# Work moved at five places of a hand-ordered layer kernel: pads, the first attention's start and steps, the second's steps and ends

## The chip, the cores and the metric

The kernel runs on one core of a Trainium2 chip. The metric is the device time of one execution in microseconds (us). Its engines are named as in the profile: PE is the matrix engine, PEld its weight loads, DVE, ACT and POOL are the vector, scalar and GpSimd engines, SP issues most DMAs.

## The reference

The inputs are x (32 batches of 112 tokens, 512 wide), a memory of 32 x 375 x 256, a mask that names one of two experts for each token, and weights. All of it is float32.

```python
# layer 0: attention over the memory, gated
memory_proj = einsum('bme,de->bmd', memory, W_mem)
attn = softmax(einsum('bnd,bmd->bnm', x, memory_proj) / sqrt(512))
context = einsum('bnm,bmd->bnd', attn, memory_proj)
gate = sigmoid(concat([x, context]) @ W_gate + b_gate)
h = rmsnorm(x + gate * context, norm_w)
# layer 1: two experts, chosen per token by vm
n = rmsnorm(h, ln_in_w)
q, k, v = split(where(vm, n @ v_qkv, n @ l_qkv))      # 16 heads of 32
ctx = softmax(causal(rope(q) @ rope(k).T)) @ v
h = h + where(vm, ctx @ v_dense, ctx @ l_dense)
cq = rmsnorm(h, ln_post_cross_w) @ cq_w               # 16 heads of 16
ck, cv = split(memory @ ckv_w)
h = h + softmax(cq @ ck.T) @ cv @ cdense_w            # 375 keys
m = rmsnorm(h, ln_post_attn_w)
return h + where(vm, v_mlp(m), l_mlp(m))              # silu(gate) * up, down
```

## The kernel before

The order of every engine is written out by hand. The blocks at the end of the program (@block.sync, gpsimd, scalar, tensor, vector) call, one after the other, a function per phase and engine (a_sp, a_pool, a_act, a_pe, a_dve, then b_..., to f_...). An instruction waits on semaphores; nothing reorders. A product of two float32 matrices is three matmuls of high and low halves (split_products, lines L111 to L113). The low halves are made by L179 on DVE or POOL.

- **Phase a** (0 to 325 us) computes layer 0 in 8 groups of 4 batches. For group g PE makes u(g), the scores, the gate products, transposes the probabilities (transposed, L681, onto PSUM) and multiplies them with the memory (attended, L689). DVE copies the turned probabilities out of PSUM (attended, L796), splits them (attended_low), blends gate and input (gated, L784 and L787) and writes the normed rows (tokens, L822). Setup work for the later routing by expert is threaded into the first groups on DVE: setup_dve_places after u_low of group 1, setup_dve_slots after the softmax of group 1. The routing sorts the 3584 tokens into 28 blocks of 128 slots plus two pad blocks: DVE computes the pads' slots in nine small instructions (L422 to L430), and POOL scatters pad rows into three tables in DRAM (L271 to L273).
- **Phase b** (to about 590 us) is the norm, qkv and rope in 8 tiles of up to 512 slots; POOL scatters the rows of q, k and v back to token order by indirect DMA (store_qk, store_v L970). The semaphore b_v_scattered counts landings of v rows. POOL waits before the last tile's scatters until all earlier ones have landed.
- **Phase c** (to about 775 us) is self-attention, one batch a step s: PE runs masks and scores (L1311, L1321) of batch s, the transposes of the probabilities (L1332) and the contexts (L1343) of batch s - 1. DVE takes maxima (L1393) and subtracts them (shift, L1402) into c_prob, ACT takes the exponent in place (L1261) and copies turned queries and keys (L1225, L1229) and turned probabilities (L1248). The first shift waits in DVE's order for the v scatters, since its destination shares their storage.
- **Phase d** is the dense product, residual and queries; phase f is the MLP in tiles.
- **Phase e** (937 to 1447 us) is cross-attention in 34 steps s. A step holds for batch s the scores (L2017, units 0 to 5, whose maxima DVE takes with L2159), for batch s - 1 the scores by key (L2038, exponents on ACT L1906), for batch s - 2 the contexts (L2051, the output in tiles of 32 columns of the array, two calls t = 0, 1), their turn (L2068) after a copy by ACT (L1912), the norm (DVE L2192, L2194), back (L2074) and the dense product. The maxima of batch s - 1 are turned by one transpose (maximum_turn, L2063), copied by DVE (L2176) and placed by a DMA of SP (L1812) into a row that the scores by key of that batch read. SP also issues the placing of keys (L1766) and queries (L1808) per batch. The key products of batch s + 2 (e_key_products) and its turned queries (queries_turn) stand in the same step.

Of the kernel before, what the change touches and what calls it, by code (L numbers as in the profile page):

```python
# [16 lines left out]
NB = 4  # L17
# [98 lines left out]
def build_xattn(nc, x_t, mem_t, mem_n, mem_e, weights, e_weights, q_weights, w_gate_mem, w_mem, b_gate,  # L116
# [3 lines left out]
    with ExitStack() as ctx:  # L120
# [137 lines left out]
        def setup_pool(pool):  # L258
            pool.memset(minus_half[:], -0.5).then_inc(s_pool, 1)
            pool.iota(row_i, pattern=[[0, SEQ]], base=0, channel_multiplier=1).then_inc(s_pool, 1)  # L260
            for m in range(RING):
                if m == C_GATE:
                    pool.wait_ge(a_m_lo, 2 * CT)
                ring_low(pool, m)
            pool.memset(tok[:, 0:PADS, :], 0.0).then_inc(pads_zeroed, 1)
            pool.wait_ge(pads_zeroed, 1)
            pool.memset(tok[:, PADS:NB, DIM:ROW], 0.0).then_inc(pads_zeroed, 1)
# [116 lines left out]
        def setup_dve_places(dve):  # L384
# [5 lines left out]
            for x, whole in enumerate((full, shift)):  # L390
                one_by_one(dve, dve.tensor_scalar(beyond[:, WHOLE * x:WHOLE * x + WHOLE], end_of, whole, None, ALU.is_gt))
            dve.wait_ge(s_rank, 2)
# [13 lines left out]
        def setup_dve_slots(dve):  # L406
# [14 lines left out]
            grid = consts[:, 8:8 + PADS]  # L421
            one_by_one(dve, dve.tensor_tensor(gap, full, count_sb, ALU.subtract))  # L422
            one_by_one(dve, dve.tensor_scalar(pads_inside, gap, -1.0, None, ALU.mult))
            one_by_one(dve, dve.tensor_tensor(pads_inside, gap, pads_inside, ALU.max))
            one_by_one(dve, dve.tensor_scalar(gap, pads_inside, -1.0, None, ALU.mult))
            one_by_one(dve, dve.tensor_scalar(pad_m, grid, pads_inside, None, ALU.is_lt))
            one_by_one(dve, dve.tensor_scalar(pad_m, pad_m, gap, float(TOKENS), ALU.mult, ALU.add))
            one_by_one(dve, dve.tensor_tensor(pad_slot[:], pad_m, grid, ALU.add))
            dve.wait_ge(pads_zeroed, 2)
            dve.tensor_scalar(tok[:, 0:PADS, ID].bitcast(I32), grid, float(TOKENS), None, ALU.add).then_inc(slots_made, 1)  # L430
# [313 lines left out]
        def a_dve(dve):  # L744
# [91 lines left out]
            for g in range(GROUPS + 1):  # L836
# [10 lines left out]
                if g < GROUPS:  # L847
                    for b in range(NB):
                        if b + 2 < NB:
                            attended(g, b + 2)  # L850
                        attended_low(g, b)
                        if g and b == 1 and g + 1 < GROUPS:
                            memory_low(g + 1, 1)
                if g:
# [4 lines left out]
                    means(g - 1, 1)  # L859
                    tokens(g - 1, 0)  # L860
# [39 lines left out]

        b_vs_last = [fv(at, (VROW,)) for at in (19248, 20336)]
# [57 lines left out]
        def b_pool(pool):  # L959
# [28 lines left out]
            pool.wait_ge(b_v_scattered, 16 * blocks(TILES - 1))  # L988
# [152 lines left out]
        c_q_t, c_k_t = ([fv(at + 448 * i, (KT, SEQ)) for i in range(2)] for at in (7728, 15872))  # L1141
        c_prob = [fv(10496 + 1792 * i, (HEADS, SEQ), SEQ) for i in range(2)]
        c_prob_t, c_ctx_raw = fv(14080, (HEADS, SEQ), SEQ), fv(16768, (KT, SEQ))
        c_tok = [fv(17216 + 512 * i, (DIM,), SEQ) for i in range(2)]
# [7 lines left out]
        def c_sp(sp):  # L1152
# [14 lines left out]
            sp.wait_ge(b_v_scattered, 16 * BLOCKS)  # L1167
# [21 lines left out]
        def c_pool(pool):  # L1189
# [5 lines left out]
            def fold(b):  # L1195
                pool.wait_ge(c_exp, b + 1)
                if b == 0:
                    pool.wait_ge(b_v_scattered, 16 * BLOCKS)
# [23 lines left out]
        def c_act(act):  # L1222
# [19 lines left out]
            for s in range(BATCHES + 1):  # L1242
# [12 lines left out]
                if s + 2 < BATCHES:  # L1255
                    keys(s + 2)
# [1389 lines left out]
```

## Time and profile before

| | us |
|---|---|
| median of 3 runs | 2146.66 |
| lowest and highest | 2146.21, 2147.8 |
| the profiled execution | 2143.99 |
| its span in the trace | 2142.2 |
| PE busy | 2093.4 (98% of the span) |
| POOL, DVE, ACT busy | 943.5, 1237.3, 1050.2 |

Of the span 1.8 us of the execution lie around it. The mean granted clock of PE on the page is 0.993. The page's last chain of waits lies on PE for 83% of the span. A wait in the trace names what ended last before an instruction could start.

### The profile page before, as it was taken

The numbers are of one execution on the slowest core, as the hardware profiler recorded it, in microseconds if no ns is written. First come the engines' busy times: TensorE is split into PE (matmuls) and PEld (weight loads), VectorE is DVE, ScalarE is ACT, GpSimd is POOL, SyncE is SP. The second block draws the span as 40 slices with busy tenths as digits, with TensorE's granted clock in tenths as the row PEclk, the third lists the DMA queues.
The fourth block names the chain that finished last, engine by engine and source line by source line (L and its number), as shares of the span: only waits on it lengthen the run. The fifth ranks groups of instructions, "written<-read, shape, count | busy, mean of one in ns | idle before, by whom it ended". The sixth has DMA issues, their size and how long they took to land.

```text
span 2142.2 us, 40674 instructions
## 1 busy us (share of the span) xinstructions
PE 2093.4 (98%) x16042; PEld 1805.2 (84%) x16042; DVE 1237.3 (58%) x1908; ACT 1050.2 (49%) x1877; POOL 943.5 (44%) x773
## 2 busy tenths in 40 slices
PE   8999999999999999999999999989999999999998
PEld 7899998888777778887888888878888888888888
DVE  6665547657589975456666666663434435344343
ACT  5444435343378865534666565553443434433334
POOL 2211127776668854551111211115455554555447
PEclk9999999999999999998999999999999999999999
DMA  6443435655666655567877777745335343443334
GB/s 248 140 158 115 144 134 177 228 204 212 212 202 181 186 189 216 227 201 212 238 235 210 226 217 222 207 132 188 116 122 174 112 140 111 131 142 118 115 89 134
DMA packets 155742, 373.00 MB, mean 174 GB/s; under 512 B 40384, under 2 KB 61216, under 8 KB 145824
## 3 DMA queue, kind: packets, MB, share of 16 engines
q1 hardware_dynamic: 136400, 310.18, 45.8%
q0 software_dynamic: 18720, 60.04, 7.6%
q8 instruction: 128, 2.10, 0.4%
q14 instruction: 62, 0.51, 0.1%
q10 hardware_dynamic: 432, 0.17, 0.0%
HBM read 268.70 MB, written 100.46 MB: 172 GB/s over the span
## 4 chain that ended last, share of the span: by engine, by line
PE 83%; DMA 5%; DVE 3%; POOL 3%; SPq 2%; ACT 2%; issue 1%; POOLq 0%; DVEq 0%; ACTq 0%
PE ps L111 20%; PE ps L113 20%; PE ps L112 20%; PE ps L2017 4%; PE ps L2038 4%; PE ps L2051 3%; PE ps L1332 2%; PE ps L689 2%; PE ps L1321 1%; PE ps L1343 1%; DMA f_arena<-weights 1%; POOL cq_rows L1569 1%; PE ps L1311 1%; DMA cq_rows<-f_arena 1%; ACT f_arena L1595 1%
## 5 line engine op out<-in xcount | busy, mean ns | idle before, releaser
L111 PE MATMUL ps<-r_arena 128*128 128x512 f32 (+6 forms) x2410 | 890.9, 370 | 14.0 <-DVE r_arena L179 8.9
L113 PE MATMUL ps<-r_arena 128*128 128x512 f32 (+6 forms) x2410 | 880.0, 365 | 0.0
L112 PE MATMUL ps<-r_arena 128*128 128x512 f32 (+6 forms) x2410 | 879.6, 365 | 0.0
L179 POOL TENSOR_TENSOR r_arena<-f_arena,r_arena 128x512 fp32r<-128x512 f32 (+1 forms) x434 | 576.7, 1353 | 542.1 <-ACT r_arena L201 397.3
L111 PEld LDWEIGHTS ps<-r_arena 128*128 128x128 f32 (+2 forms) x2410 | 453.1, 188 | 79.0 <-POOL r_arena L179 6.7
L113 PEld LDWEIGHTS ps<-r_arena 128*128 128x128 f32 (+2 forms) x2410 | 452.7, 188 | 64.9
L112 PEld LDWEIGHTS ps<-r_arena 128*128 128x128 f32 (+2 forms) x2410 | 453.7, 188 | 59.3
L201 ACT CAST r_arena<-f_arena 128x512 fp32r<-128x512 f32 x400 | 236.4, 624 | 172.5 <-PE ps L113 127.3
L2159 DVE TENSOR_REDUCE e_negmax<-ps 112x3 f32<-112x1125 f32 (+1 forms) x192 | 229.9, 1198 | 113.1 <-PE ps L2017 113.0
L2476 DVE SCALAR_TENSOR_TENSOR f_arena<-f_arena,ps 128x512 f32<-128x512 f32 (+1 forms) x88 | 57.5, 653 | 233.8 <-ACT f_arena L2363 233.8
L1906 ACT ACTIVATE f_arena<-ps 125x896 f32<-125x896 f32 x192 | 165.4, 915 | 35.6 <-PE ps L2038 33.0
L2367 ACT CAST r_arena<-ps 128x512 fp32r<-128x512 f32 (+1 forms) x88 | 49.3, 561 | 240.1 <-DVE ps L2480 240.1
L1864 POOL DMA_INDIRECT cd_rows<-f_arena,slot_all x32 | 30.0, 937 | 268.2 <-ACT f_arena L1961 268.0
L2017 PE MATMUL ps<-r_arena 96*112 96x376 f32 x512 | 134.6, 358 | 9.7 <-DVE e_negmax L2159 4.5
L179 DVE TENSOR_TENSOR r_arena<-ps,r_arena 128x512 fp32r<-128x512 f32 (+2 forms) x186 | 102.6, 563 | 71.6 <-ACT r_arena L2367 55.1
L2480 DVE SCALAR_TENSOR_TENSOR ps<-f_arena,ps 128x512 f32<-128x512 f32 (+1 forms) x88 | 58.3, 663 | 103.9 <-PE ps L113 103.6
L2363 ACT ACTIVATE f_arena<-ps 128x512 f32<-128x512 f32 (+1 forms) x88 | 50.2, 571 | 133.0 <-PE ps L113 133.0
L2038 PEld LDWEIGHTS ps<-r_arena 98*125 98x125 f32 x768 | 99.5, 192 | 15.3 <-ACT f_arena L1906 9.9
L2038 PE MATMUL ps<-r_arena 98*125 98x224 f32 x768 | 110.4, 281 | 1.8 <-DMA r_arena<-r_arena 0.8
L2017 PEld LDWEIGHTS ps<-r_arena 96*112 96x112 f32 x512 | 81.9, 184 | 24.9 <-DVE e_negmax L2159 13.7
L518 POOL TENSOR_TENSOR a_rstd<-a_ss,minus_half 112x2 f32<-112x2 f32 x16 | 11.3, 705 | 194.8 <-DVE a_ss L806 194.7
L1202 POOL TENSOR_TENSOR f_arena<-f_arena 112x896 f32<-112x896 f32 x32 | 66.9, 2090 | 34.6 <-ACT f_arena L1261 32.7
(215 smaller groups left out, 2575.4 us busy)
## 6 DMA issues: line engine op xcount, KB each, us to landing
f_arena<-weights SPq DMA_DIRECT2D x400, 256.0 KB, 3.0
r_arena<-k_rows SPq DMA_DIRECT2D x192, 188.0 KB, 3.6
k_rows<-r_arena SPq DMA_DIRECT2D x64, 376.0 KB
f_arena<-rows SPq DMA_DIRECT2D x14, 1160.0 KB, 5.2
f_arena<-qk_rows SPq DMA_DIRECT2D x32, 448.0 KB, 4.1
f_arena<-mem_n SPq DMA_DIRECT2D x8, 1536.0 KB, 6.8
f_arena<-mem_e SPq DMA_DIRECT2D x32, 376.0 KB, 4.9
f_arena<-mem_t SPq DMA_DIRECT2D x16, 750.0 KB, 5.5
```

What stands on the lines that cost most here:

```text
L111: first = pe.matmul(out, w_hi, x_hi, start=start, stop=False)
L112: pe.matmul(out, w_hi, x_lo, start=False, stop=False)
L113: return first, pe.matmul(out, w_lo, x_hi, start=False, stop=stop)
L179: return engine.tensor_tensor(out, source, high.bitcast(F32), ALU.subtract)
L201: act.copy(w_hi[:, m % RING, :], w_raw[:, m % RING, :]).then_inc(w_hi_made, 1)
L1202: pool.tensor_tensor(c_half, c_prob[b % 2][:, :, 0:half], c_prob[b % 2][:, :, half:SEQ], ALU.add).then_inc(c_halved.sem, 1)
L1906: act.activation(e_pt[:, u], ps[0:KC, at:at + 2, 0:4 * SEQ], ACT.Exp).then_inc(e_exp, 1)
L2017: last = pe.matmul(ps[0:SEQ, s_bank(b, u) + h - s_heads[u][0], 0:CEVEN], e_queries[b % 3][0:MAX_ROW, h % 2, h // 2, :], e_keys[b % 3][0:MA ...
L2038: last = pe.matmul(ps[0:KC, 4 + 2 * (u % 2) + n // 2, n % 2 * 2 * SEQ:(n % 2 + 1) * 2 * SEQ], e_keys[b % 3][0:MAX_ROW + 2, pair, m], e_que ...
L2051: last = pe.matmul(ps[32 * a:32 * a + 32, 3, batch(n)], e_cv[b % 4][:, c, 4 * n + a, :], e_pt[:, NKC * t + c, half, batch(a)], start=c == ...
L2159: dve.tensor_reduce(e_negmax[:, b % 2, heads[0]:heads[-1] + 1], ps[0:SEQ, s_bank(b, u):s_bank(b, u) + len(heads), 0:CTX], AX_X, ALU.max, n ...
L2480: dve.scalar_tensor_tensor(ps[:, bank + 1, w], act_a[:, s, w], 0.5, ps[:, bank + 1, w], ALU.mult, ALU.mult).then_inc(f_glu_made, 1)
```

## The change

Six edits, none of which adds or drops arithmetic:

1. Phase a: the nine DVE instructions of the pads' slots go from setup_dve_slots into setup_dve_places, POOL's two memsets go ahead of the ring chunk that waits for a_m_lo, so both stand earlier. In the first group DVE copies the turned probabilities of group 1 ahead of the first gate blend (t = 0) and between later blends, no longer before the last blend. For g = 1 the split of the memory (memory_low) goes behind tokens(0, 0) and means(0, 1).
2. Phase b to c: the last tile's v scatters count on a semaphore of their own; POOL no longer waits before them. The two homes of c_prob are swapped and four other homes shift by 16, so that the wait of the first shift for the v scatters stands before the second (b == 1).
3. Phase c: ACT's exponent of batch s stands ahead of its copy of the keys of batch s + 2, in every step.
4. Start of phase e: in step 1 the key products of batch 3 stand half before and half after the first scores, the turned queries of batch 3 before the scores of unit 2; scores(0, 5) go to PSUM bank 2.
5. Every step of phase e: maximum_turn(s - 1) stands between the two contexts of batch s - 2, no longer behind both.
6. End of phase e: in the steps of the last two batches DVE's norm stands ahead of the maximum of unit 1; four of the six query placements of batch 31 are issued on ACT's queue; the first residual addition of phase f (f_add) is split in two.

```diff
 setup_dve_places:
+            (the nine pad instructions L422 to L430, from setup_dve_slots)
 a_dve, gated(g):
+                copies = KT - 1 if g else 0
...
-                    if t == KT - 1 and g + 1 < GROUPS:
+                    if t == copies and g + 1 < GROUPS:
                         for b in range(2):
                             attended(g + 1, b)
...
+                    if g == 0 and t in (1, 2):
+                        attended(1, t + 1)
 a_dve, group g = 1:
+                    if g == 1:
+                        tokens(g - 1, 0)
+                        means(g - 1, 1)
+                        memory_low(g + 1, 1)
 b_pool:
-                    pool.indirect_dma_start(v_rows, ids, b_values(n, j), None).then_inc(b_v_scattered, 16)
+                    done = b_v_scattered if n + 1 < TILES else b_last_scattered.sem
+                    pool.indirect_dma_start(v_rows, ids, b_values(n, j), None).then_inc(done, 16)
...
-            pool.wait_ge(b_v_scattered, 16 * blocks(TILES - 1))
             store_v(TILES - 1)
 c_dve, shift(b):
-                if b == 0:
+                if b == 1:
                     dve.wait_ge(b_v_scattered, 16 * blocks(TILES - 1))
 c_act:
-                if s + 2 < BATCHES:
-                    keys(s + 2)
...
                     act.activation(c_prob[s % 2], c_prob[s % 2], ACT.Exp, scale=float(HD) ** -0.5).then_inc(c_exp, 1)
+                if s + 2 < BATCHES:
+                    keys(s + 2)
 e_pe:
+                if s == 1:
+                    e_key_products(pe, 3, (0,))
                 if now:
                     scores(s, 0)
+                if s == 1:
+                    e_key_products(pe, 3, (1,))
                 if old:
                     context(s - 2, 0)
...
+                if by_key:
+                    maximum_turn(s - 1)
+                if old:
                     context(s - 2, 1)
...
-                if by_key:
-                    maximum_turn(s - 1)
 e_dve:
-                if s < BATCHES:
+                if s < BATCHES and s not in last_two:
                     maximum(s, 1)
...
                 if s >= 2:
                     norm(s - 2)
+                if s in last_two:
+                    maximum(s, 1)
 e_act:
+                    if s == BATCHES - 2:
+                        act.wait_ge(e_st, KEY_UNITS * (BATCHES - 3))
+                        place_last(act, last_places[2:])
```

How PE's instructions stand in a step of phase e, before; L2051 are the contexts of batch s - 2, L2063 is the turn of the maxima, L2068 that of the copied context:

```order
L2038 MATMUL ps<-r_arena 125x224 x8
L2017 MATMUL ps<-r_arena 112x376 x3
L2051 MATMUL ps<-f_arena 32x112 x48
L2063 MATMUL ps<-ident,r_arena 128x112
L2017 MATMUL ps<-r_arena 112x376 x3
L2068 MATMUL ps<-ident,f_arena 112x128 x4
```

And after, where the same lines are numbered L2080 (contexts), L2092 (maxima) and L2097 (turn):

```order
L2067 MATMUL ps<-r_arena 125x224 x8
L2046 MATMUL ps<-r_arena 112x376 x3
L2080 MATMUL ps<-f_arena 32x112 x24
L2092 MATMUL ps<-ident,r_arena 128x112
L2080 MATMUL ps<-f_arena 32x112 x24
L2046 MATMUL ps<-r_arena 112x376 x3
L2097 MATMUL ps<-ident,f_arena 112x128 x4
```

An order row counts an instruction of float32 once that the trace counts twice, so 24 here are 48 there. The one transpose has moved from behind the contexts to between their two halves; what follows on PE is the same.

How DVE's instructions stand in group 0 to 1 of phase a, before; L784 and L787 are the two halves of a gate blend, L796 the copies of probabilities:

```order
L434 TENSOR_TENSOR f_arena<-f_arena 128x1
L784 SCALAR_TENSOR_TENSOR f_arena<-f_arena 128x448
L787 SCALAR_TENSOR_TENSOR f_arena<-f_arena 128x448
L179 TENSOR_TENSOR r_arena<-f_arena,r_arena 128x1500
L784 SCALAR_TENSOR_TENSOR f_arena<-f_arena 128x448
L787 SCALAR_TENSOR_TENSOR f_arena<-f_arena 128x448
L784 SCALAR_TENSOR_TENSOR f_arena<-f_arena 128x448
L787 SCALAR_TENSOR_TENSOR f_arena<-f_arena 128x448
L796 COPY f_arena<-ps 125x336 x2
L784 SCALAR_TENSOR_TENSOR f_arena<-f_arena 128x448
L787 SCALAR_TENSOR_TENSOR f_arena<-f_arena 128x448
L796 COPY f_arena<-ps 125x336
```

And after, where the blend is L786 and L789 and the copy L800:

```order
L435 TENSOR_TENSOR f_arena<-f_arena 128x1
L800 COPY f_arena<-ps 125x336 x2
L786 SCALAR_TENSOR_TENSOR f_arena<-f_arena 128x448
L789 SCALAR_TENSOR_TENSOR f_arena<-f_arena 128x448
L179 TENSOR_TENSOR r_arena<-f_arena,r_arena 128x1500
L786 SCALAR_TENSOR_TENSOR f_arena<-f_arena 128x448
L789 SCALAR_TENSOR_TENSOR f_arena<-f_arena 128x448
L800 COPY f_arena<-ps 125x336
L786 SCALAR_TENSOR_TENSOR f_arena<-f_arena 128x448
L789 SCALAR_TENSOR_TENSOR f_arena<-f_arena 128x448
L800 COPY f_arena<-ps 125x336
```

The first two copies have moved ahead of all blends, the other two behind the second and third; the split of 1500 columns stays between the first and second blend.

## Rows read from the trace of the kernel before

**Rows 1.** Page, part 1: engine, busy us (share of the span), instructions.

```profile
PE 2093.4 (98%) x16042; PEld 1805.2 (84%) x16042; DVE 1237.3 (58%) x1908; ACT 1050.2 (49%) x1877; POOL 943.5 (44%) x773
```

**Rows 2.** Waits of PE, 55 to 110 us (us, times, longest).

```profile
PE ps L689 <- DVE f_arena L796: 3.8, 1, 3.8
```

**Rows 3.** Timeline of DVE, phase a (start, length, what).

```profile
61.95 0.16 DVE L422 TENSOR_TENSOR f_arena<-f_arena 128x1 f32<-128x1 f32 x1
```

**Rows 4.** Windows, 71.5 to 74.9 us: five engines busy, then granted clock.

```profile
71.50:74.90 3.40, 3.40 (x19) 3.40 (x18) 0.92 (x3) 1.75 (x3) 0.86 (x1) 0.50 0.80 249
```

**Rows 5.** DMA issues in 55 to 95 us: count, KB, median us to landing.

```profile
f_arena<-x_t SPq DMA_DIRECT2D x1, 896.0 KB, 8.9
```

**Rows 6.** DMA issues in 108 to 120 us.

```profile
f_arena<-x_t SPq DMA_DIRECT2D x1, 896.0 KB, 4.3
```

**Rows 7.** Timeline of DVE before the third group of phase a.

```profile
81.12 2.23 DVE L179 TENSOR_TENSOR r_arena<-f_arena,r_arena 128x448 fp32r<-128x448 f32 x4 [1.19 <-ACT r_arena L538]
...
83.80 2.73 DVE L822 SCALAR_TENSOR_TENSOR f_arena<-ps,a_rstd,norm 112x512 f32<-112x512 f32 x4
```

**Rows 8.** Waits of PE in 330 to 600 us.

```profile
PE ps L1311 <- DVE f_arena L1402: 1.7, 2, 1.3
PE ps L1343 <- DMA f_arena<-v_rows: 0.8, 1, 0.8
```

**Rows 9.** Timeline of POOL, the last scatters of phase b.

```profile
593.11 0.96 POOL L970 DMA_INDIRECT v_rows<-f_arena  x1 [0.31 <-issue]
```

**Rows 10.** Timeline of ACT around the start of phase c.

```profile
590.87 0.59 ACT L1232 COPY f_arena<-ps 128x512 f32<-128x512 f32 x1 [4.01 <-PE ps L113]
```

**Rows 11.** Timeline of ACT in one step of phase c.

```profile
648.04 0.53 ACT L1229 COPY f_arena<-ps 128x448 f32<-128x448 f32 x1
648.47 1.70 ACT L1261 ACTIVATE f_arena<-f_arena 112x1792 f32<-112x1792 f32 x1
650.07 0.61 ACT L1265 CAST r_arena<-f_arena 128x512 fp32r<-128x512 f32 x1
650.86 1.40 ACT L1248 COPY f_arena<-ps 112x448 f32<-112x448 f32 x3 [0.17 <-PE ps L1332]
```

**Rows 12.** Waits of PE in 937 to 1015 us.

```profile
PE ps L2017 <- DVE e_negmax L2159: 3.9, 4, 1.2
```

**Rows 13.** Windows, 979.5 to 986.3 us.

```profile
979.50:986.30 6.80, 6.73 (x76) 5.87 (x78) 3.43 (x5) 3.10 (x4) 0.00 (x0) 0.50 0.75 240
```

**Rows 14.** Timeline of PE in one step of phase e.

```profile
1239.99 2.51 PE L2051 MATMUL ps<-f_arena 125*32 125x112 f32 x96
1242.43 0.32 PE L2063 MATMUL ps<-ident,r_arena 112*128 112x112 f32 x1
1242.52 0.74 PE L2017 MATMUL ps<-r_arena 96*112 96x376 f32 x3
1243.15 0.65 PE L2068 MATMUL ps<-ident,f_arena 128*112 128x128 f32 x4
1243.56 0.42 PE L111 MATMUL ps<-r_arena 128*128 128x376 f32 x1
```

**Rows 15.** Waits of PE in 1015 to 1395 us.

```profile
PE ps L2017 <- DMA r_arena<-q_rows: 0.4, 2, 0.2
```

**Rows 16.** Line L2068, 1015 to 1400 us: what ended idle before it.

```profile
  ACT f_arena L1912: 5.6, 26
```

**Rows 17.** Timeline of PE, end of phase e.

```profile
1443.50 1.36 PE L2051 MATMUL ps<-f_arena 125*32 125x112 f32 x48
1444.79 0.66 PE L2382 MATMUL ps<-ident,f_arena 128*128 128x128 f32 x4
1445.37 1.36 PE L2051 MATMUL ps<-f_arena 125*32 125x112 f32 x48
```

**Rows 18.** Waits of PE in 1395 to 1450 us.

```profile
PE ps L2074 <- DVE f_arena L2194: 2.8, 3, 1.0
PE ps L2017 <- DMA r_arena<-q_rows: 1.4, 1, 1.4
```

More of the change, by code:

```diff
@@ L391, in setup_dve_places @@
                 one_by_one(dve, dve.tensor_scalar(beyond[:, WHOLE * x:WHOLE * x + WHOLE], end_of, whole, None, ALU.is_gt))
+            grid = consts[:, 8:8 + PADS]
+            one_by_one(dve, dve.tensor_tensor(gap, full, count_sb, ALU.subtract))
+            one_by_one(dve, dve.tensor_scalar(pads_inside, gap, -1.0, None, ALU.mult))
+            one_by_one(dve, dve.tensor_tensor(pads_inside, gap, pads_inside, ALU.max))
+            one_by_one(dve, dve.tensor_scalar(gap, pads_inside, -1.0, None, ALU.mult))
+            one_by_one(dve, dve.tensor_scalar(pad_m, grid, pads_inside, None, ALU.is_lt))
+            one_by_one(dve, dve.tensor_scalar(pad_m, pad_m, gap, float(TOKENS), ALU.mult, ALU.add))
+            one_by_one(dve, dve.tensor_tensor(pad_slot[:], pad_m, grid, ALU.add))
+            dve.wait_ge(pads_zeroed, 2)
+            dve.tensor_scalar(tok[:, 0:PADS, ID].bitcast(I32), grid, float(TOKENS), None, ALU.add).then_inc(slots_made, 1)
             dve.wait_ge(s_rank, 2)
@@ L848, in a_dve @@
                     for b in range(NB):
-                        if b + 2 < NB:
+                        if b + 2 < NB and g != 1:
                             attended(g, b + 2)
                         attended_low(g, b)
-                        if g and b == 1 and g + 1 < GROUPS:
+                        if g >= 2 and b == 1 and g + 1 < GROUPS:
                             memory_low(g + 1, 1)
@@ L858, in a_dve @@
                         x_low(g + 1)
-                    means(g - 1, 1)
-                    tokens(g - 1, 0)
+                    if g == 1:
+                        tokens(g - 1, 0)
+                        means(g - 1, 1)
+                        memory_low(g + 1, 1)
+                    else:
+                        means(g - 1, 1)
+                        tokens(g - 1, 0)
                     tokens(g - 1, 1)
@@ L1140, in build_xattn @@
         c_v = [fv(6144 + VROW * i, (HEADS, HD), SEQ) for i in range(3)]
[L1141 to L1144, printed above, removed]
+        c_q_t, c_k_t = ([fv(at + 448 * i, (KT, SEQ)) for i in range(2)] for at in (7728, 15888))
+        c_prob = [fv(12304 - 1792 * i, (HEADS, SEQ), SEQ) for i in range(2)]
+        c_prob_t, c_ctx_raw = fv(14096, (HEADS, SEQ), SEQ), fv(16784, (KT, SEQ))
+        c_tok = [fv(17232 + 512 * i, (DIM,), SEQ) for i in range(2)]
         c_turn_banks = (4, 5, 7)
@@ L1166, in c_sp @@
                 load_qk(b)
-            sp.wait_ge(b_v_scattered, 16 * BLOCKS)
+            sp.wait_ge(b_v_scattered, 16 * blocks(TILES - 1))
+            sp.wait_ge(*b_last_scattered.at(16 * tb(TILES - 1)))
             for b in range(3):
@@ L1484, in e_key_products @@
             if b >= 3:
-                pe.wait_ge(e_kq_lo, e_split(b - 1))
+                pe.wait_ge(e_kq_lo, e_split(b - 1 if b > 3 else 1))
+            if b == 3:
+                pe.wait_ge(e_maxed, S_UNITS - 2)
             if b >= 4:
@@ L1772, in place_queries, with place_last @@
                     e_placed[b].sem, 16)
+        def place_last(engine, parts):
+            b = BATCHES - 1
+            engine.wait_ge(*stored(b))
+            into, done = e_queries[b % 3].rearrange("p t g s -> p t (g s)").bitcast(F32), e_placed[b % 2].sem
+            for t, part in parts:
+                engine.dma_start(rows_of(into, t, part)[:, t], q_rows[b, t, (0, 0, 1)[part]]).then_inc(done, 16)
+        last_places = [(t, part) for t in range(CT) for part in range(3)]
         def e_sp(sp):
@@ L1804, in place_both @@
                 place_keys(sp, b)
+                if b == BATCHES - 1:
+                    place_last(sp, last_places[:2])
+                    return
                 into, done = e_queries[b % 3].rearrange("p t g s -> p t (g s)").bitcast(F32), e_placed[b % 2].sem
@@ L2116, in e_pe @@
                     scores(s, 2)
-                if new and s:
+                if s == 1:
+                    queries_turn(3)
+                if new and s >= 2:
                     e_key_products(pe, s + 2)
@@ L2124, in e_pe @@
                     scores(s, 2)
-                    queries_turn(s + 2)
+                    if s != 1:
+                        queries_turn(s + 2)
                     if s >= 2:
@@ L2215, in e_dve @@
                     maximum_turned(s - 1)
-                if s < BATCHES:
+                if s == BATCHES:
+                    f_add(dve, 0, (2, 3))
+                if s < BATCHES and s not in last_two:
                     maximum(s, 1)
@@ L2430, in f_pe, with f_add @@
                 project_down(tile, FT - 1)
-        def f_add(dve, tile):
+        def f_add(dve, tile, parts):
             dve.wait_ge(*f_h_loaded[tile % 3].at(16 * (tile // 3 + 1)))
             dve.wait_ge(*f_cd_loaded.at(16 * (tile + 1)))
-            for j in range(tb(tile)):
+            for j in parts:
                 x = f_x[tile % 3][:, j, 0:DIM]
@@ L2484, in f_dve @@
                     if i == 5 and tile + 1 < TILES:
-                        f_add(dve, tile + 1)
+                        f_add(dve, tile + 1, range(tb(tile + 1)))
                     if i == 7 and tile + 1 < TILES:
```

25 lines of the change are left out of this document (9 added, 16 removed).

## The prediction

> **What bounds the kernel now.** I read the page's busy times first: PE is busy for 98% of the span [rows 1], so a change counts where PE waits, where its clock is down, or where its own stream gets longer. Then the waits of PE, stage by stage, for the places that the change touches: 3.8 us in the first groups of phase a [rows 2], 1.7 and 0.8 us at the passage from b to c [rows 8], 3.9 us for the maxima at the start of phase e [rows 12], 0.4 us in all its regular steps [rows 15], 2.8 and 1.4 us at its end [rows 18]. Those are the sums that can be gained. The regular steps of e are full; what is put between their matmuls is paid on the spot. The granted clock, in the windows, is 0.50 (the lower level of 1.2 GHz) behind the wait in phase a [rows 4] and again at the start of e [rows 13].
>
> **The change part by part.** All is summed against the profiled execution, 2143.99 us, and then moved to the median of the runs, which lies 2.67 us above it.
>
> *Phase a.* PE's wait of 3.8 us is for the copies of turned probabilities (L796) [rows 2], which DVE reaches only after three blends. In the new order two copies stand ahead of all blends and the others between them, so they are done before PE asks, and the wait goes. The stretch at half clock that follows it, 3.40 us of it busy [rows 4], would be half as long: 1.7 us more. Against this stand the nine pad instructions, now ahead of a softmax that PE's scores wait for: nine of 0.16 us are 1.4 us [rows 3] at most, nothing where DVE would stand idle; I take 1.0. So PE would be up to 3.8 + 1.7 - 1.0 = 4.5 us early. What is late next is the product u(2), behind the tokens (L822), behind the split of x (L179, which sat idle for x's high half), behind the load of x [rows 7]. That load took 8.9 us, among the pad scatters; the same load one group later, without them, took 4.3 [rows 5, 6]. The pads' slots are now ready a whole softmax earlier, and POOL, which waited for them, scatters the pads before x is loaded, so I take 4.3: 4.6 us won, less the 1.0 us by which it is issued later, is -3.6. If it still takes 8.9 us, phase a is +1.0; if the load isn't the limit, -4.5.
>
> *From b to c.* The last v scatter was issued at 593.11 [rows 9], since POOL first waited for the landing of the others. Its data was there at 590.87 + 0.59 = 591.46 [rows 10]. Issued then, its rows land 1.65 us sooner; the first subtraction, whose wait in DVE's order is now one batch later, no longer waits, which removes the 1.7 us before L1311, and the values that PE's first contexts wait for 0.8 us come sooner by the same 1.65 [rows 8]. The two lie on one chain: -1.6, between -0.8 (only the second shrinks) and -2.5 (both go).
>
> *Steps of c.* The exponent starts with no idle time before it, though the copy of the keys stands ahead [rows 11]: it was released by DVE about then, so nothing is won in the regular step. The copy now stands behind. It holds ACT from 648.04 to 648.47, 0.43 us; where a cast (L1265) also stands there, in 15 steps, the probability copies that follow had 0.17 us of idle time [rows 11], so they start up to 0.26 us later. The loop of PE, DVE and ACT closes over two steps, so I price 0.07 us a step: +1.1. Ends: 0 and 15 x 0.26 / 2 = +2.0.
>
> *Start of e.* Half of the key products of batch 3 stands ahead of the first scores of batch 1, and fills one of the four waits for maxima, 1.2 us of 3.9 [rows 12]; DVE's chain of maxima is no shorter, so the other three stay. -1.2; at best -3.9, and +1.2 if the products only push that chain back by one such wait.
>
> *Every step of e.* This is the large term. In a step the 96 records of contexts (48 of each call) run from 1239.99 to 1242.43, when the transpose of the maxima starts; it takes PE 0.09 us before the next scores begin at 1242.52 [rows 14]. The turn L2068 then starts at 1243.15, and in 26 of 26 steps it sits idle until ACT's copy of the contexts has ended (5.6 us in all) [rows 16]. That copy can start only when the last context is done. With the transpose between the halves the last context is done later, and nothing can absorb it: the turn is already what waits, and the scores between are there in either order. How much later? The last step shows two context calls apart, with transposes between [rows 17]: the first half holds PE for 1443.50 to 1444.79, 1.29 us, where two halves together hold 2.44, so one more exit from the 32-column tiles costs 2 x 1.29 - 2.44 = 0.14. The four transposes there hold it for 0.58, four before an ordinary matmul for 1243.56 - 1243.15 = 0.41 [rows 14, 17], so the entry costs 0.17. The transpose itself, 0.09 today, lies now ahead of the copy. Ends: 0.14 + 0.09 = 0.23 without the entry, 0.14 + 0.09 + 0.17 = 0.40 with all of it. I take the middle, 0.32, since neither row is of this transpose alone. From step 2 to 29 that is 28 x 0.32 = +9.0 (6.4 to 11.2). What the earlier transpose gives back (the copy L2176 and the placing of the maxima sooner) is of use only to scores by key, which wait for nothing in these steps [rows 15].
>
> The Trainium skill speaks against this part too (TensorEngine Tiling (Array Packing), Key Properties): changing the tiling mode, and not just the tile, drains the engine. It gives no figure; by it two more drains a step come with the transpose, and by the rows above those are 0.14 and 0.17, so by that rule the sum is the upper end, 11.2.
>
> *End of e.* The wait of 1.4 us for the queries of batch 31 [rows 18] goes when ACT's queue issues four of the six. The three 1.0 us or shorter waits for the norm (2.8) shrink where it stands ahead of a maximum, but the maximum is then late for the scores that need its bank, so I count nothing. Three steps with the split contexts cost 3 x 0.32 = 1.0. Sum -0.4, between -1.4 - 2.8 + 1.0 = -3.2 and +2.3 (1.0, and one maximum of the size of the 1.2 us waits).
>
> *The sum.* -3.6 - 1.6 + 1.1 - 1.2 + 9.0 - 0.4 = +3.3 us: 2147.3 for a profiled execution, 2146.66 + 3.3 = 2150.0 for the median.
>
> **The rivals.** *The transpose costs nothing between the contexts.* For it: 0.09 us is all it takes today, and the idle time before the turn could be PE's own change of form, not a wait for ACT. Against it: the two context calls apart in the last step, and 26 of 26 idle times that end with ACT's copy. Then the sum is 3.3 - 9.0 - 1.0 = -6.7, 2140.0.
>
> *The clock comes back at the start of e.* Between 979.5 and 986.3 PE is busy for 6.73 us at half clock [rows 13], 3.4 us of them lost. If the key products, moved into the waits, keep the clock up, the sum is -0.1, 2146.6. Against it: only one wait of four is filled, and the half clock there begins after waits that stay.
>
> *The load of x stays slow*, the case on the slower side. Its place is the third group of phase a; its price is the 4.6 us that I counted as won, so 3.3 + 4.6 = +7.9, 2154.6. For it: the loads of the memory, which follow on the same queues, also shared that stretch, and they stay. Against it: the 4.3 us of the next group had those beside it too. It decides from a load of about 5.3 us on: beyond that each us is a us of the end, and with the steps' 9.0 the kernel is slower by more than can be taken for none.
>
> **How the numbers follow.** What a measurement of this kernel can tell from no change is about 0.2%, 4.3 us. My forecast has 0.60, the free transpose 0.17, the clock 0.10, the slow load 0.13. The forecast's terms spread by some 3.5 us about +3.3, mostly from the 6.4 to 11.2 of the steps; so of its 0.60 some 0.23 lies above +4.3 and 0.36 within. Slower: 0.23 + 0.13 = 0.36. Faster: most of the free transpose, 0.14, and 0.02 from the tails: 0.16. The same: 0.48. The range: below, to within the free transpose, 2141.0; above, to the slow load, 2154.6. For the forecast alone it is 2145.5 to 2154.
>
> **What would show it.** Phase a: no wait of 3.8 us before L689's successor, full clock at 71.5 to 75, a load of x of 4 to 5 us, and the tokens (L822) at about 80.2 in place of 83.8 [rows 7]. B to c: the last scatter at 591.5 plus phase a's shift, first contexts 1.6 us sooner relative to it. Steps of e: a step longer by 0.2 to 0.4 us, with the time between the first context and L2068's counterpart longer by the same, and again idle until ACT's copy in every step. The prediction is wrong if that interval doesn't grow, if the load of x stays at 9 us, or if the low clock at the start of e is gone.

## The result: 0.26% slower, and the profile after

| | before | changed |
|---|---|---|
| median of 10 runs, us | 2145.80 | 2152.56 |
| ratio, 95% interval | | 1.0026 [1.0017, 1.0036] |
| span of the profiled execution, us | 2142.2 | 2148.2 |

The forecast was 2150.0 by a sum of +3.3 us. The ratio is worth +5.6 us (interval 3.6 to 7.7), the medians differ by 6.8 and the two profiled spans by 6.0. One execution of the first kernel in experiment 7 took 9906.13 us and enters no ratio. By the spans, four stretches got shorter, and of those that got longer one did so by far the most. The landmarks are starts of PE's instructions in the two traces.

| stretch | before | changed | difference | forecast |
|---|---|---|---|---|
| start to the last idle time of phase a | 325.31 | 321.73 | -3.6 | -3.6 |
| from there to the first contexts of phase c | 273.40 | 271.17 | -2.2 | -1.6 |
| first to last contexts of phase c | 189.48 | 190.43 | +1.0 | +1.1 |
| from there to the first scores of phase e | 169.61 | 168.94 | -0.7 | 0 |
| first scores to the turn of batch 0 | 30.20 | 29.92 | -0.3 | -1.2 |
| turn of batch 0 to turn of batch 28 | 419.91 | 430.42 | +10.5 | +9.0 |
| turn of batch 28 to that of batch 31 | 40.94 | 42.31 | +1.4 | -0.4 |
| from there to PE's end | 687.37 | 687.39 | 0.0 | 0 |

The page of the changed kernel, part 1, beside [rows 1]: PE's busy time grew by 13.0 us, more than the span.

```profile
PE 2106.4 (98%) x16042; PEld 1805.5 (84%) x16042; DVE 1235.6 (58%) x1908; ACT 1049.7 (49%) x1877; POOL 945.4 (44%) x773
```

Phase a. The longer of the two waits of PE from 50 to 110 us in the changed kernel (us, times, longest), now for the tokens; the wait of 3.8 us for copies [rows 2] is gone:

```profile
PE ps L111 <- DVE f_arena L826: 1.5, 1, 1.5
```

The window that stood at half clock before [rows 4] is at full clock, and the load of x took 4.8 us where it took 8.9 [rows 5]. A window's row, then the row of DMA issues from 50 to 95 us:

```profile
71.50:74.90 3.40, 3.40 (x32) 3.40 (x32) 2.23 (x8) 3.32 (x8) 0.00 (x0) 1.00 0.45 124
```

```profile
f_arena<-x_t SPq DMA_DIRECT2D x1, 896.0 KB, 4.8
```

The timeline of DVE shows the split of x and the first two tokens, 3.5 and 4.0 us sooner than in [rows 7]:

```profile
77.66 2.23 DVE L179 TENSOR_TENSOR r_arena<-f_arena,r_arena 128x448 fp32r<-128x448 f32 x4 [2.28 <-ACT r_arena L539]
79.81 1.41 DVE L826 SCALAR_TENSOR_TENSOR f_arena<-ps,a_rstd,norm 112x512 f32<-112x512 f32 x2
```

From b to c. The timeline of POOL has the last scatter of v at 587.24 (593.11 before, 3.6 us of which are phase a's) [rows 9], and PE's waits from 330 to 600 us have none left for the subtraction [rows 8]. The wait for the values (L1343 before, L1355 now) is still there and longer, 1.2 us for 0.8:

```profile
587.24 0.96 POOL L981 DMA_INDIRECT v_rows<-f_arena  x1 [3.01 <-ACT f_arena L1244]
```

```profile
PE ps L1355 <- DMA f_arena<-v_rows: 1.2, 1, 1.2
```

A third wait, for the first rows of queries and keys, stood there before (waits of PE from 330 to 600 us) and is also gone:

```profile
PE ps L1295 <- DMA f_arena<-qk_rows: 0.8, 1, 0.8
```

Every step of e. The timeline of PE in a step of the changed kernel, to be laid beside [rows 14] (L2080 are the contexts, L2092 the maxima, L2046 scores, L2097 the turn):

```profile
1240.01 1.36 PE L2080 MATMUL ps<-f_arena 125*32 125x112 f32 x48
1241.30 0.32 PE L2092 MATMUL ps<-ident,r_arena 112*128 112x112 f32 x1
1241.55 1.36 PE L2080 MATMUL ps<-f_arena 125*32 125x112 f32 x48
1242.83 0.78 PE L2046 MATMUL ps<-r_arena 96*112 96x376 f32 x3
1243.56 0.65 PE L2097 MATMUL ps<-ident,f_arena 128*112 128x128 f32 x4
```

The contexts began at 1240.01 and were over at 1242.83, 2.82 us, where 2.44 were enough; the parts are 1.29, 0.25 and 1.28. From the first context to the turn it is 3.54 us, 3.16 before, in the median of the regular steps. From the start of the last context to the turn it is 0.91 us in both: the turn follows the last context at the same distance, whether the transpose stands between the two or not. The turn is still released by ACT's copy (line L2097 from 1015 to 1400 us, us and times):

```profile
  ACT f_arena L1938: 7.0, 25
```

Start and end of e. The windows of the changed kernel (busy times as in [rows 13], then the clock) show two stretches at the lower level, 6.8 and 10.2 us; before they were 13.7 and 6.8 long:

```profile
956.20:963.00 6.80, 5.87 (x18) 4.49 (x17) 4.76 (x8) 0.00 (x0) 0.00 (x0) 0.50 0.69 161
...
969.90:980.10 10.20, 10.03 (x79) 8.59 (x78) 4.32 (x6) 5.35 (x6) 0.00 (x0) 0.50 0.84 241
```

At the end the wait for the queries of batch 31 [rows 18] is gone, and the scores by key wait for a maximum; the wait for the norm (L2074 before, L2103 now) is 1.4 us for 2.8 (waits of PE from 1395 to 1456 us):

```profile
PE ps L2067 <- DVE e_negmax L2196: 2.1, 2, 1.0
PE ps L2103 <- DVE f_arena L2231: 1.4, 3, 0.8
```

Another wait of the kernel before (1395 to 1450 us) is gone as well, that of the scores by key (L2038) for the row of maxima that a DMA places:

```profile
PE ps L2038 <- DMA r_arena<-r_arena: 0.8, 2, 0.6
```

### The profile page after: what moved, and what is told of

It reads as the page before. It is cut to its first block, busy times and chain, and to the rows that moved or that the text cites. A ratio compares the mean times of both kernels' runs of the same rounds, so it can differ in the third digit from the quotient of the medians.

```text
span 2148.2 us, 40677 instructions
## 1 busy us (share of the span) xinstructions
PE 2106.4 (98%) x16042; PEld 1805.5 (84%) x16042; DVE 1235.6 (58%) x1908; ACT 1049.7 (49%) x1877; POOL 945.4 (44%) x773
## 4 chain that ended last, share of the span: by engine, by line
PE 85%; DVE 5%; DMA 4%; ACT 2%; POOL 2%; issue 1%; SPq 1%; POOLq 0%; DVEq 0%; ACTq 0%
PE ps L111 20%; PE ps L113 20%; PE ps L112 20%; PE ps L2046 5%; PE ps L2067 4%; PE ps L2080 4%; PE ps L690 2%; PE ps L1344 2%; DVE c_max L1405 1%; DMA f_arena<-weights 1%; DVE f_arena L1414 1%; POOL cq_rows L1583 1%; PE ps L1333 1%; DMA cq_rows<-f_arena 1%; PE ps L2097 1%
## 5 line engine op out<-in xcount | busy, mean ns | idle before, releaser
L111 PE MATMUL ps<-r_arena 128*128 128x512 f32 (+6 forms) x2410 | 890.3, 369 | 15.5 <-DVE r_arena L179 8.8
L111 PEld LDWEIGHTS ps<-r_arena 128*128 128x128 f32 (+2 forms) x2410 | 452.8, 188 | 80.4 <-POOL r_arena L179 6.8
L201 ACT CAST r_arena<-f_arena 128x512 fp32r<-128x512 f32 x400 | 236.4, 624 | 172.0 <-PE ps L113 125.3
L2046 PE MATMUL ps<-r_arena 96*112 96x376 f32 x512 | 135.8, 359 | 6.4 <-DVE e_negmax L2196 4.8
L2067 PEld LDWEIGHTS ps<-r_arena 98*125 98x125 f32 x768 | 101.0, 194 | 17.5 <-ACT f_arena L1932 10.9
L2046 PEld LDWEIGHTS ps<-r_arena 96*112 96x112 f32 x512 | 79.8, 180 | 26.6 <-DVE e_negmax L2196 14.6
L2080 PE MATMUL ps<-f_arena 125*32 125x112 f32 x3072 | 88.0, 263 | 0.0
```

Source lines behind the costliest of these rows:

```text
L111: first = pe.matmul(out, w_hi, x_hi, start=start, stop=False)
L201: act.copy(w_hi[:, m % RING, :], w_raw[:, m % RING, :]).then_inc(w_hi_made, 1)
L2046: last = pe.matmul(ps[0:SEQ, s_bank(b, u) + h - s_heads[u][0], 0:CEVEN], e_queries[b % 3][0:MAX_ROW, h % 2, h // 2, :], e_keys[b % 3][0:MA ...
L2067: last = pe.matmul(ps[0:KC, 4 + 2 * (u % 2) + n // 2, n % 2 * 2 * SEQ:(n % 2 + 1) * 2 * SEQ], e_keys[b % 3][0:MAX_ROW + 2, pair, m], e_que ...
L2080: last = pe.matmul(ps[32 * a:32 * a + 32, 3, batch(n)], e_cv[b % 4][:, c, 4 * n + a, :], e_pt[:, NKC * t + c, half, batch(a)], start=c == ...
```

## The experiments

In diffs of the kernel before, lines are of that kernel; what an experiment takes over from the change is named.

**1. The transpose back behind both contexts, all else changed.**

```diff
 e_pe, the changed kernel:
                     context(s - 2, 0)
...
-                if by_key:
-                    maximum_turn(s - 1)
-                if old:
                     context(s - 2, 1)
...
+                if by_key:
+                    maximum_turn(s - 1)
```

> The changed kernel with the transpose of the maxima back behind both contexts; all else as changed. Theory (the transpose between the contexts changes PE's tile form twice and lies ahead of ACT's copy, which the turn waits for): the step falls from 15.37 us to 14.98, 28 steps give back 10.5 us and the last three about 1; span about 2136.6, ratio to before about 0.997. Rival (another edit lengthened the steps, the exponent's or the placements' order): the step stays at 15.3 to 15.4 and the span near 2148.

Measured: 2142.0 us, ratio to before 0.9975 [0.9966, 0.9984]. The step is 14.99 us, and from the first context to the turn it is again 3.16. Against the 1.0026 of the changed kernel that is 0.51%, 10.9 us, where 11.5 were expected. The span of its one profile, 2141.9, is 5.3 above the expected 2136.6. Of this, 3.3 us lie ahead of the first turn of e (0.8 in phase a, 0.3 to the first contexts of c, 1.4 from c to e, 0.8 behind it), where the edit leaves PE's order as it was. The clock was down for 27.4 us at the start of e, 17.0 in the changed kernel's profile, which can be a part of it. The end of e took 43.39 us, 1.1 more than in the changed kernel where about 1 less was expected; PE waited there for 2.6 us for the row of maxima. Without this edit the change is a gain.

**2. The transpose between the contexts, all else as before.**

```diff
 e_pe, the kernel before:
                     context(s - 2, 0)
...
+                if by_key:
+                    maximum_turn(s - 1)
+                if old:
                     context(s - 2, 1)
...
-                if by_key:
-                    maximum_turn(s - 1)
```

> The kernel before with only the transpose of the maxima between the two contexts. Theory: the step grows from 14.98 to 15.36 us, 28 steps and the last three cost 11.5 us: span about 2153.7, ratio 1.0054. Rival (another edit lengthened the steps): the step stays at 14.98, span 2142.

Measured: 2157.95 us, 1.0047 [1.0034, 1.0061], a step of 15.37 us. The edit costs by itself what it costs in the change: 10.5 us in the 28 regular steps, 0.38 each. No other edit lengthened them.

**3. The transpose in the contexts' form.** The changed kernel, with the 112 x 128 transpose cut into four matmuls with the identity, each into a tile of 32 columns:

```diff
 maximum_turn, the changed kernel:
-                pe.transpose(ps[:, 7, CDIM:CDIM + SEQ], e_max_tok[b % 2].bitcast(F32), ident[0:SEQ, 0:SEQ])
+                for a in range(4):
+                    last = pe.matmul(ps[32 * a:32 * a + 32, 7, CDIM:CDIM + SEQ],
+                                     e_max_tok[b % 2][:, 32 * a:32 * a + 32].bitcast(F32),
+                                     ident[0:SEQ, 0:SEQ], start=True, stop=True)
```

> The changed kernel, where the transpose between the contexts is made by four matmuls with the identity in tiles of 32 columns, the form of the contexts. Theory (two changes of form cost most of the 0.38 us): no change of form is left; four such matmuls take as long as four of the contexts, 2.44 / 12 = 0.20 us, so the step falls from 15.37 to about 15.18 and 28 steps give back 5.3 us: span about 2142.5. Rival (whatever stands between the contexts costs by its wait and its length, the form has no part): four matmuls where one stood are no shorter, the step stays at 15.37 or grows by 0.1 to 15.47, span 2148 to 2151.

Measured: 2145.66 us, 1.0000 [0.9989, 1.0011], and a step of 15.18 us. The timeline of PE in a step (L2093 are the four matmuls, eight records; the scores L2046 begin when the contexts L2080 are over):

```profile
1239.31 0.38 PE L2093 MATMUL ps<-ident,r_arena 112*32 112x112 f32 x8
1239.51 1.33 PE L2080 MATMUL ps<-f_arena 125*32 125x112 f32 x48
1240.77 0.77 PE L2046 MATMUL ps<-r_arena 96*112 96x376 f32 x3
```

The four matmuls hold PE from 1239.31 to 1239.51, 0.20 us, and the step is longer than before by just that. Each record there has a 112 x 32 tile, where the transpose had 112 x 128. Four matmuls in the contexts' form cost 0.19 us a step less than one transpose in another, so at least half of the 0.38 was the two changes of form, as long as the transpose alone is no more work than the four (it takes 0.09 us behind the contexts [rows 14]). The rest goes with the place: from the start of the last context to the turn it is 0.91 us here too, as in experiments 1 and 2, so whatever stands between the contexts delays the turn by its whole length.

**4. The copies of phase a without the pads.** The kernel before, with the copies and the split of the memory (memory_low, cut from the lines shown) moved as in the change, and the pads' slots and scatters left where they were:

```diff
 gated(g), the kernel before:
+                copies = KT - 1 if g else 0
...
-                    if t == KT - 1 and g + 1 < GROUPS:
+                    if t == copies and g + 1 < GROUPS:
...
+                    if g == 0 and t in (1, 2):
+                        attended(1, t + 1)
...
```

> The kernel before with the half of the first edit that moves the copies of the probabilities (and the split of the memory behind the tokens); the pads' slots and scatters stay where they were. Theory (behind the removed wait stands the load of x, slow only beside the pad scatters): the wait of 3.8 us is gone and so is the half clock behind it, but x is loaded at about 71.5 and takes 8 to 9 us again, so the first tokens come at 83 to 84 and phase a ends within 1 us of the kernel before (its last idle time on PE at 324.5 to 326, 325.3 before, 321.7 in the changed kernel). Rival (the copies alone do it, the load is no limit): phase a ends 3 to 4.5 us sooner, at 321 to 322.

Measured: phase a's last idle time is at 327.24, 1.9 us later than in the kernel before, where it was expected within 1 us; one run of 2148.39 us. In the seven profiles with neither half of the edit it lies at 324.7 to 327.1 (mean 325.7), in the five with both at 321.4 to 322.5 (mean 322.0). So the copies alone gain nothing, and a loss isn't clear of the spread. The waits of PE from 55 to 110 us, and the load of x:

```profile
PE ps L111 <- DVE f_arena L825: 4.3, 1, 4.3
PE ps L111 <- DVE r_arena L179: 1.6, 1, 1.6
```

```profile
f_arena<-x_t SPq DMA_DIRECT2D x1, 896.0 KB, 7.8
```

The 3.8 us came back as 4.3 and 1.6, and the clock fell behind them. The timeline of DVE shows a second thing that I had not priced: the names of the tokens (L816) wait for the landing of the pad scatters.

```profile
80.51 0.29 DVE L816 COPY f_arena<-cos_sin 112x256 f32<-112x256 f32 x1 [4.23 <-DMA cd_rows<-f_arena,pad_slot]
...
82.26 2.23 DVE L179 TENSOR_TENSOR r_arena<-f_arena,r_arena 128x448 fp32r<-128x448 f32 x4 [0.28 <-ACT r_arena L538]
```

They started at 80.51, and the split of x at 82.26, so both the late load and the late scatters keep the tokens. The copies earn only with the pads moved; the pads alone were not tested.

**5. Passage from b to c, with and without the exponent's move.** Two kernels: the second and third edit; and the second alone. The semaphore of the last scatters and the homes of the probabilities move in both and are cut from the lines shown.

```diff
 the kernel before, b_pool and c_dve (both kernels):
-            pool.wait_ge(b_v_scattered, 16 * blocks(TILES - 1))
             store_v(TILES - 1)
...
-                if b == 0:
+                if b == 1:
                     dve.wait_ge(b_v_scattered, 16 * blocks(TILES - 1))
...
 c_act (the first kernel only): keys(s + 2) behind the exponent
```

> The kernel before with the second and third edit alone (semaphore of the last v scatters, homes of the probabilities, exponent ahead of the keys). Theory: PE's first contexts of self-attention start 2.2 us sooner than in the kernel before (598.71), at 596.5, and the last ones too, by 2.0 to 2.3, since the exponent's place is neutral in the steps. Rival (my forecast for the steps): up to 1.1 us of it is lost again by the last contexts of phase c.

> The kernel before with the second edit alone (the exponent stays behind the copy of the keys). Theory: first contexts of self-attention 2.2 to 2.4 us sooner after the end of phase b, and 189.5 us from there to the last contexts as before, where the second and third edit together took 190.44: the exponent's move costs 0.95 us. Rival (the swapped homes cost it): 190.4.

Measured: with both edits the first contexts start at 597.05, 27.63 us behind the last wait of PE for POOL in phase b, where it was 30.04 before: 2.4 us won. From the first to the last contexts it is 190.44 us with the exponent's move and 189.65 without it (189.48 before). So the move costs 0.8 to 1.0 us, not nothing as expected of the first kernel, and the swapped homes nearly nothing. Over all profiles it is 190.43 to 190.55 in the four kernels with the move and 189.47 to 189.67 in the nine without. In the second kernel the first contexts start 28.18 us behind that wait, 1.9 us won; so the exponent's move adds 0.5 us here in the first step and loses nearly twice that in the others.

The parts show where. The subtraction's wait, 1.7 to 2.6 us in the six kernels without the second edit, is in none of the seven with it; the wait for the values is 0.9 to 1.4 us in these seven, 0 to 0.8 in the six. The wait for queries and keys comes and goes in both groups (0 to 0.8 and 0 to 0.2), so its part in the pair's 2.2 us is not shown to be the edit's. At this passage, from 592 to 601 us, the clock fell for 3.4 to 6.8 us in four of the six, and in none of the seven. In the steps of c, the changed kernel takes about 5.87 and 6.06 us by turns where it was 5.97 in each step, which comes to nothing, but the 15 steps of 640 to 730 us, in which ACT's 14 casts stand (L1265, L1267 and L201 before), lose 1.1 us.

**6. The start of e alone.**

```diff
 e_pe, the kernel before:
+                if s == 1:
+                    e_key_products(pe, 3, (0,))
                 if now:
                     scores(s, 0)
+                if s == 1:
+                    e_key_products(pe, 3, (1,))
...
```

> The kernel before with the fourth edit alone (key products of batch 3 around the first scores, start of cross-attention). Theory: from the first scores to the first scores by key 17.3 us in place of 18.8, but half a clock longer behind it, so that the first turn comes 0 to 1.5 us sooner after the first scores than before (30.2 us); ratio 0.999 to 1.000. Rival (the clock's stretch in the changed kernel was chance): the whole 1.5 us stay, 28.7 us.

Measured: 0.9997 [0.9987, 1.0007]; 17.47 us to the first scores by key and 29.53 to the first turn, between the two expectations. Over all profiles, from the first scores to the first turn the six kernels with this edit took 29.5 to 31.3 us (mean 30.3), the seven without it 30.0 to 32.3 (mean 31.4). In each of them the clock was down for 17 to 27 us there. The two groups overlap, but between kernels with the same time at the lower level the edit's are shorter in the mean: by 0.4 us at 20.5, 0.7 at 23.9 and 1.4 at 27.3. To the scores by key it was 17.3 to 17.8 us with it and 18.3 to 19.9 without.

**7. The end of e alone, and its placements alone.**

```diff
 e_dve, the kernel before (first kernel only):
-                if s < BATCHES:
+                if s < BATCHES and s not in last_two:
                     maximum(s, 1)
...
+                if s in last_two:
+                    maximum(s, 1)
 e_act (both kernels):
+                    if s == BATCHES - 2:
+                        act.wait_ge(e_st, KEY_UNITS * (BATCHES - 3))
+                        place_last(act, last_places[2:])
...
```

> The kernel before with the sixth edit alone (norm ahead of a maximum, queries of batch 31 on ACT's queue, residual addition split). Theory: the wait of 1.4 us for the queries goes, but the scores by key wait about 1.0 us in two steps for the maximum that is now behind the norm, and the clock drops once more (1.7 us): from the turn of batch 28 to that of batch 31 41 to 41.5 us, 40.94 before; ratio 1.000. Rival (those 1.4 us come from the transpose between the contexts, the edit by itself gains): 39.5 to 40 us.

> The kernel before with four of the six query placements of batch 31 on ACT's queue, and nothing else of the sixth edit. Theory: the wait of 1.4 us for them is gone; from the turn of batch 28 to that of batch 31 39.5 to 40 us with one drop of the clock, 41 to 42 with two; ratio 0.999 to 1.000. Rival (issuing on ACT delays its casts): 41 to 42 with one drop.

Measured: 1.0009 [0.9998, 1.0019] for the whole edit, with 43.84 us from the turn of batch 28 to that of batch 31; 0.9996 [0.9986, 1.0005] for the placements alone, with 40.78. But kernels whose end nothing touched took 40.8 to 44.2 us there. The clock was down for 3.4 to 10.2 us in them, and the wait for the row of maxima varied from 0.5 to 3.5 us, so this stretch by itself decides nothing; in the first kernel here that wait was 3.1 us, in the second 1.1. The swap of norm and maximum earned nothing: PE's waits for the norm, the maxima and the exponent sum to 3.4 us in the kernel before (2.8 and 0.6) and to 3.4 with the whole edit (1.7, 1.0 and 0.7). Whether it costs anything beyond that stays open.

**8. What was worth keeping.** The first, second and fourth edit on the kernel before, nothing else of the change. The places of phase a, the scatters of b, the first subtraction of c and step 1 of e stand as changed; ACT's exponent in c, the transpose of the maxima, the query placements, norm and maximum, and f_add stand as before.

> The kernel before with the first, second and fourth edit alone: without the exponent's move, the transpose between the contexts and the edits at the end. Theory: phase a 3.6 us, the passage to self-attention 2.4, the start of cross-attention 1.2 us sooner, steps of both attentions as before (189.5 us from the first to the last contexts of self-attention, 14.99 a step of cross-attention): 7.2 us less, ratio 0.9967. Rival (the gains hang on each other or on the exponent's move): less than half of it, ratio over 0.998.

Measured: 2138.07 us, 0.9964 [0.9952, 0.9976], as summed. This beats both kernels.

**9. The wait before the turn filled.** The kernel of 8, with one quarter of the key products ahead of the turn:

```diff
 e_pe, the kernel of 8:
+                if new and s >= 2:
+                    e_key_products(pe, s + 2, trios=(0,))
                 if old:
                     turn(s - 2)
...
-                    e_key_products(pe, s + 2)
+                    e_key_products(pe, s + 2, trios=(1, 2, 3))
```

> The kernel kept, with one new move: in each step of cross-attention from the third on, the first three of the twelve matmuls of the key products stand ahead of the turn. Theory (the turn waits 0.21 us a step for ACT's copy, and whatever lies behind the copy's wait is paid in full): three matmuls of 0.17 us fill that wait, the step falls from 14.99 to about 14.78, 28 steps give 5.9 us, ratio to before about 0.994. Rival (the turn, 0.3 us later, makes the norm and what follows late by as much, or the idle time is only PE's change of form): the step stays at 14.99 to 15.1, ratio 0.9967 as kept.

Measured: 2136.17 us, 0.9958 [0.9944, 0.9971]; against the kernel of 8 the intervals overlap. Most steps take 14.87 us, 0.12 less, not 0.21; two others lost 1.1 us together to late queries. The timeline of PE (L2033 are the scores, L111 begins the key products):

```profile
1235.36 0.74 PE L2033 MATMUL ps<-r_arena 96*112 96x376 f32 x3
1235.94 0.34 PE L111 MATMUL ps<-r_arena 128*128 128x376 f32 x1
```

The product behind the three scores starts 0.58 us after the first of them. The turn, in its place before, started 0.63 after it [rows 14]. So only some 0.05 us was a wait that other work could have used; the rest of the 0.21 that the line's row showed as idle time [rows 16] was PE's own tail of the scores. What else the 0.12 us came from was not tested.

## Why the prediction was right, and where a size was off

The sign, the bounds of all six terms, and the mechanism of the largest term held. The total came out larger: by the spans +6.0 us for +3.3. Of the 2.7 us between them the steps of e are 1.5, the end of e 1.8 and its start 0.9, against 0.6 at the passage from b to c and 0.7 from c to e. The stretch from c to e was put at nothing and no edit touches it; it took 168.4 to 171.5 us over the thirteen profiles. The chances were less right than the sum: 0.48 for a change of less than 4.3 us either way, 0.36 for a slower kernel, and what came, 5.6 us with an interval of 3.6 to 7.7, lies mostly in the second. Point by point:

- **Phase a** came as summed, -3.6, and -3.7 in the means over all profiles. What I named as late next was right: the tokens behind the split and the load of x. The load took 8.9 and 7.8 us with the pad scatters beside it (experiment 4) and 4.8 without. The loads of the memory do not explain it: SP issued one (mem_t) 4.4 to 4.9 us ahead of x in all three kernels, and the next (mem_n) 6.4 us behind it in the kernel before, 0.5 in experiment 4 and 1.0 in the changed kernel, where the load of x was fast. That DVE's names also wait for those scatters I had not seen.
- **From b to c** -2.2 to -2.4 for -1.6, within the range but by other parts. The subtraction's wait went, 1.7 us, as said. The wait for the values was to shrink and got longer instead, 1.2 us for 0.8. The 0.8 us wait for queries and keys, which I had not listed, was gone too: 1.7 + 0.8 - 0.3 (1.18 for 0.84) is the pair's 2.2. The size was partly luck.
- **Steps of c** +0.8 to +1.0 for +1.1, shown by experiment 5, and lost where I had put it, in the steps with the casts and over pairs of steps.
- **Every step of e** was the mis-sized term: 0.38 us a step for 0.32, 10.5 for 9.0. The step that failed is "I take the middle, 0.32, since neither row is of this transpose alone". The rows for the two changes of form (0.14 and 0.17) held nearly whole: 1.29 + 0.25 + 1.28 against 2.44. Experiment 3 shows that the changes of form are at least half of it. That the transpose's own 0.09 is paid too, since the turn waits for ACT's copy, fits the 0.91 us from the last context to the turn in either order; of the idle time that I read as this wait, 0.21 us a step, experiment 9 leaves some 0.05. The Trainium skill's rule (TensorEngine Tiling (Array Packing), Key Properties), that changing the tiling mode drains the engine, would have given the upper end, 11.2, which was nearer than my middle.
- **Start of e** -0.3 in this pair for -1.2, and about -1.1 in the mean over all profiles: the gain is there, and the clock moves it by more than its size.
- **End of e** +1.4 for -0.4. The wait for queries went as said. The norm's waits fell from 2.8 to 1.4 us, and in return the scores by key waited 2.1 us for maxima (0.6 before, in other scores) and 0.7 for the exponent; all waits of PE there sum to 5.1 us, 6.0 before. Three steps of the large term cost 3 x 0.38 = 1.1. What I did not count is the clock: it was down for 6.8 us, 3.4 before, with PE busy throughout, which is up to 1.7 us more; that this is an effect of the change is not shown. I also overlooked what the earlier transpose gives back here: the ten kernels with it behind the contexts wait for 0.5 to 3.5 us for the row of maxima at the end of e, the three with anything of it between them not at all.

Of the rivals, the free transpose is refuted by experiments 1 to 3, though one of its reasons, that the idle time before the turn is mostly PE's own, is borne out by experiment 9. The slow load didn't come but is real (experiment 4), and the clock at the start of e did not come back: it was down for 17.0 us, 20.5 before.

## What to carry to other kernels

In a stream that is 98% busy, ask of every instruction that is moved whose release lies behind it: one short transpose put ahead of a copy that a later instruction waits for was paid 31 times. Price both the way out of the matrix engine's tile form and the way back: here the sum of the two rows, 0.40 with the transpose itself, was nearer to the 0.38 measured than the middle. And look at an edit's parts one by one: three of the six were worth 0.36%, and one took it all back.

## What was not expected of the hardware

The stretches at the lower clock at the start of cross-attention differ between kernels that are the same up to there: 20.5 us in all in the kernel before, 27.3 and 23.9 in the first and second kernel of experiment 7, which touch only the end. Without the fourth edit, the stretch from the first scores to the first turn took 30.0 to 30.2 us where the clock was down for 20.5 us, and 31.8 to 32.3 where it was down for 27.3. The time of an execution goes with the clock granted over all of it: of 57 executions of the kernel before that were taken beside the experiments (2141.18 to 2151.93 us), the seven with a mean clock of 0.989 took 2148.8 us in the mean, the fourteen with 0.992 took 2144.3. The intervals between landmarks in a stretch at full clock repeat far better: the regular step was 14.98 to 15.00 us in all nine kernels with the old order and no other change to the step, and 15.37 in both with the new one.
